# Tile loads of 192 rows on 64 partitions, in alternate halves of TensorE's rows, in a two-layer graph kernel

## The chip, the cores and the metric

The kernel runs on one core of a Trainium2 chip. The metric is the device time of one execution in microseconds; lower is better.

## What is computed

A graph network with two layers over 50,000 nodes and 50,000 edges, 128 channels, all in float32. The edges are sorted by destination.

```python
h = relu(layernorm(x))
# layer 0: edge features, message, sum over edges, MLP on nodes
ef  = ssp(gaussians(edge_weight) @ Wf1 + bf1) @ Wf2 + bf2      # ssp(v) = softplus(v) - log 2
agg = segment_sum((h @ W_lin.T)[src] * ef, dst, N)
x   = x + ssp(agg @ Wm1 + bm1) @ Wm2 + bm2
# layer 1: own row and the mean over neighbours
h   = relu(layernorm(x))
neigh = h[dst] @ W_neigh.T + b_neigh
x   = x + h @ W_self.T + b_self + segment_sum(neigh, src, N) / max(count(src), 1)
```

## The kernel before

The rows are padded to 98 quads of 512 rows; a quad is four tiles of 128. There are three stages. A short first stage counts and ranks the edges. The middle stage is one software pipeline, `over_steps`, of 98 + 18 steps. In step s each engine works on several quads at once: the edge part of quads s to s-3, the node part of quads s-7 to s-12, and the edge rows for layer 1 of quads s-15 to s-18. The last stage sums the rows of layer 1 by source.

The change is in the middle stage. Two groups of products there sum rows by a one-hot matrix that VectorE makes:

- `block_sums` (L1049) adds the messages of one tile of 128 destinations. SyncE loads 256 consecutive rows of the message table into `win`, two rows on each of 128 partitions, and `one_hots` (L821) makes `hot`. For each of the four tiles there are two products of 128 x 128 x 128, eight in all.
- `edge_rows` (L1061) picks for each edge the row of its destination from 256 rows in `hwin` by means of `hotT` (`edge_hots`, L849), again eight products.

Both write the same PSUM bank (`agg_ps` is also `rows_ps`). ScalarE copies it out in `evacuate` to `aggs` and in `rows_out` (L978). A float32 product of 128 columns stands in the trace as two records, each with its own weight load.

The order of work inside a step is written out by hand in each engine's `step`, and each engine goes through its list strictly in that order; semaphores hold it back. On TensorE (L1072) it is: self product of s-11, `block_sums` of s-8, MLP product of s-9, node product with Wm1, neighbour product of s-11, `filter_up` of s (50 rows of the edge basis by Wf1), `edge_rows` of s-17, transposes of s-10, `wlin` product of s-2, filter product and transposes of s-1. `product` begins with one matmul of 3 rows that adds the bias.

Three waits matter in what follows. `filter_up` of quad s writes the bank that `soften` has still to read for quad s-1, so it waits for that `soften` (output `su`). On VectorE (L863) this `soften` of s-1 stands late in step s: behind `node_out` of s-11 (L842, output `ys` or `y_kept`), `row_keys`, small operations and the four instructions of `node_norm` (output `comb`). And `node_out` of s-11 waits for the self product of s-11, with which TensorE begins the same step s.

Of the kernel before, what the change touches and what calls it, by code (L numbers as in the profile page):

```python
# [8 lines left out]
C = 128  # L9
P = 128  # L10
QT = 4
# [9 lines left out]
SPAN = 2 * P  # L21
# [127 lines left out]
def gnn_kernel(nc, ins, out_dram):  # L149
# [5 lines left out]
    with ExitStack() as ctx:  # L155
# [62 lines left out]
        iota2 = consts[:, 3 * P + 7:3 * P + 9]  # L218
        qbase = sb("qbase", [P, QUADS])
        firsts = sb("firsts", [P, TILES])  # L220
# [5 lines left out]
        reach = sb("reach", [P, TILES, 2])  # L226
# [4 lines left out]
        weights += [(qbase, "qbase"), (iota4, "iota4")]  # L231
# [39 lines left out]
        with ExitStack() as sems:  # L271
# [63 lines left out]
            @block.sync  # L335
            def _(sp):
                for t, a in ((cur[:], ins["dst_flat"][0:ROWS].rearrange("(p t) -> p t", p=P)),
                             (nxt[:], ins["dst_flat"][1:ROWS + 1].rearrange("(p t) -> p t", p=P)),
                             (ends[:, 0, :], ins["tile_first"].partition_broadcast(P)),
                             (ends[:, 1, :], ins["tile_last"].partition_broadcast(P)),  # L340
                             (first_row[0:1, :], ins["tile_first"].unsqueeze(0))):
                    sp.dma_start(t, a).then_inc(dst_loaded, 16)
                sp.dma_start(consts[:], ins["consts"]).then_inc(consts_loaded, 16)
                for t, name in weights:
                    sp.dma_start(t[:], ins[name]).then_inc(weights_loaded, 16)
                for t, name in rows:
# [4 lines left out]
                sp.dma_start(msg_dram[ROWS:ROWS + SPAN, :].rearrange("(p w) c -> p (w c)", p=P), pads[:, 0:2 * MW]).then_inc(pads_set, 16)  # L351
                sp.dma_start(h1_dram[ROWS:ROWS + SPAN, :].rearrange("(p w) c -> p (w c)", p=P), pads[:, 0:2 * C]).then_inc(pads_set, 16)
                sp.wait_ge(starts_ready, 1)
                sp.dma_start(off_dram.rearrange("(h l) -> h l", h=HI), starts[:]).then_inc(starts_out, 16)
                sp.wait_ge(starts_out, 16)
                sp.dma_start(start_row[0:1, :], off_dram.unsqueeze(0)).then_inc(starts_in, 16)
                sp.wait_ge(starts_in, 16)
                sp.wait_ge(pads_set, 16 * 3)
                sp.wait_ge(weights_loaded, 16 * (len(weights) + len(rows)))

            @block.vector
            def _(dve):
# [41 lines left out]
                for w in range(2):  # L404
                    nc.vector.tensor_scalar(reach[:, :, w], firsts[:], iota2[:, w:w + 1], None, ALU.add)
# [159 lines left out]
        rel = sb("rel", [P, QT, 2])  # L565
# [9 lines left out]
        with nc.If(unfit == 0), ExitStack() as fast:  # L575
# [9 lines left out]
            with ExitStack() as sems:  # L585
# [9 lines left out]
                win = st("win", [P, 2, QT, 2, MW])  # L595
                hwin = st("hwin", [P, 2, QT, 2, C])
                hot = st("hot", [P, QT, 2, P])
                hotT = st("hotT", [P, QT, 2, P])
                row_out = st("row_out", [P, 2, QT, RW])
                msgw = st("msgw", [P, 2, QT, MW])  # L600
                dst_keys = st("dst_keys", [P, 2, QROWS], i32)
# [24 lines left out]
                u_ps, turn_ps, proj_ps, filt_ps, agg_ps, nu_ps, mlp_ps, self_ps = bank  # L626
                neigh_ps, rows_ps = self_ps, agg_ps
# [4 lines left out]
                def _(sp):  # L632
# [29 lines left out]
                    def load_windows(j, par):  # L662
# [11 lines left out]
                        for k, start in enumerate(starts_of):  # L674
                            sp.dma_start(win[:, par, k, :, :].rearrange("p w c -> p (w c)"),
                                         msg_dram[bass.ds(start, SPAN), :].rearrange("(p w) c -> p (w c)", p=P)).then_inc(win_loaded[par], 16)

                    def load_keys(q, par):
                        if not at_first(q, 2):
                            sp.wait_ge(x_hot, q - 1)  # L680
                            hold(sp, sp_passed)
                        sp.dma_start(dst_keys[:, par, :], ins["dst_rows"][q, :].partition_broadcast(P)).then_inc(x_keys[par], 16)

                    def load_hidden(q, par):
# [11 lines left out]
                        for t, first in enumerate(firsts_of):  # L696
                            sp.dma_start(hwin[:, par, t, :, :].rearrange("p w c -> p (w c)"),
                                         h1_dram[bass.ds(first, SPAN), :].rearrange("(p w) c -> p (w c)", p=P)).then_inc(x_win[par], 16)
# [57 lines left out]
                def _(dve):  # L756
# [59 lines left out]
                    def window_dst(j, par):  # L816

                        dve.wait_ge(win_loaded[par], half_count(j, par, 64))
                        nc.vector.tensor_scalar(rel[:], win[:, par, :, :, C], qbase[:, bass.ds(j, 1)], None, ALU.subtract).then_inc(n_rel, 1)

                    def one_hots(j):  # L821

                        dve.wait_ge(n_rel, j + 1)
                        wait_used(dve, n_agg, j, 1)
                        nc.vector.tensor_tensor(hot[:], iota4[:].rearrange("p (t c) -> p t c", t=QT).unsqueeze(2).broadcast_to([P, QT, 2, P]),  # L825
                                                rel[:].unsqueeze(3).broadcast_to([P, QT, 2, P]), ALU.is_equal).then_inc(n_hot, 1)
# [22 lines left out]
                    def edge_hots(q, par):  # L849

                        dve.wait_ge(x_keys[par], half_count(q, par, 16))
                        wait_used(dve, x_sum, q, 1)
                        nc.vector.tensor_tensor(hotT[:], dst_keys[:, par, :].rearrange("p (t e) -> p t e", t=QT).unsqueeze(2).broadcast_to([P, QT, 2, P]),  # L853
                                                reach[:, bass.ds(QT * q, QT), :].unsqueeze(3).broadcast_to([P, QT, 2, P]), ALU.is_equal).then_inc(x_hot, 1)
# [8 lines left out]
                    def step(s, even, odd, pair, slot, late):  # L863
                        if there(s - 8):
                            one_hots(s - 8)
# [59 lines left out]
                def _(act):  # L925
# [52 lines left out]
                    def rows_out(q, par):  # L978
# [4 lines left out]
                        nc.scalar.activation(row_out[:, par, :, 0:C], rows_ps[:].rearrange("p (t c) -> p t c", t=QT), ACT.Copy).then_inc(x_rows, 1)  # L983

                    nc.scalar.preload_act_table_set("natural_log_exp_and_others")  # L985
                    def step(s, even, odd, pair, slot, late):
                        if there(s - 9):
                            evacuate(s - 9, aggs[:], agg_ps[:], n_agg, n_u, n_aggT)
# [7 lines left out]
                        if there(s - 9):  # L996
                            clamp(s - 9, nu_ps[:], bm1_top, nclamp[:], n_u, n_clamp)
                        if there(s - 11):
                            evacuate(s - 11, nhT[:], turn_ps[:], n_turned, n_neigh, n_hT, ACT.Relu)
                        if there(s - 12):  # L1000
                            hidden_out(s - 12, even)
                        if there(s - 18):
                            rows_out(s - 18, even)
# [22 lines left out]
                def _(pe):  # L1026
# [22 lines left out]
                    def block_sums(j, par):  # L1049
# [3 lines left out]
                        if there(j - 10):  # L1053
                            pe.wait_ge(x_rows, j - 10 + 1)
                        for k in range(QT):
                            for w in range(2):
                                last = nc.tensor.matmul(agg_ps[:, k * P:(k + 1) * P], win[:, par, k, w, 0:C], hot[:, k, w, :],  # L1057
                                                        start=(w == 0), stop=(w == 1))
                        last.then_inc(n_agg, 1)

                    def edge_rows(q, par):  # L1061
# [4 lines left out]
                        for t in range(QT):  # L1066
                            for w in range(2):
                                last = nc.tensor.matmul(rows_ps[:, t * P:(t + 1) * P], hotT[:, t, w, :], hwin[:, par, t, w, :],  # L1068
                                                        start=(w == 0), stop=(w == 1))
# [1023 lines left out]
```

## Time and profile before

| what | us |
|---|---|
| median of 3 runs | 1956.16 (1955.95 to 1958.92) |
| the profiled execution, its own time | 1953.39 |
| its span | 1950.9 |
| steps 17 to 97 of the middle stage, in the span | 402.66 to 1468.32 |
| TensorE busy, share of the span | 90% |
| VectorE, ScalarE, GpSimd busy | 77%, 54%, 52% |

The span is what the profile shows of the execution. A step's length is read as the distance from one bias matmul of the self product to the next. Busy shares are averages over stages; which engine bounds a step is read from the timeline of that step.

### The profile page before, as it was taken

How to read it: one execution, taken by the hardware profiler on the slowest of the kernel's cores; microseconds unless marked ns; L12 is line 12 of the kernel's file. 1: busy time of each engine (PE TensorE's matmuls, PEld its weight loads, DVE VectorE, ACT ScalarE, POOL GpSimd, SP SyncE). 2: the span in 40 equal slices, each digit the busy share in tenths (PEclk: the TensorE clock that was granted, in tenths of full speed). 3: DMA queues.
4: the chain of work that ended last, by engine and by line, in shares of the span. 5: the costliest groups of instructions: out<-in, count | busy, mean ns of one | idle time of the engine just before them, and what ended most of it. 6: DMA issues, size and time to landing. Idle time of an engine off the chain costs nothing. (4 is left out here: it accounts for less than half of the span.)

```text
span 1950.9 us, 46269 instructions
## 1 busy us (share of the span) xinstructions
PE 1751.3 (90%) x11686; PEld 1336.5 (69%) x11686; DVE 1495.5 (77%) x4726; ACT 1062.0 (54%) x2453; POOL 1021.4 (52%) x886
## 2 busy tenths in 40 slices
PE   2639868999999999999999999999999864988997
PEld 1212236777777777777777777777777754888897
DVE  8989946887778778777877777787787624777886
ACT  1000067777777777777777777777775311333333
POOL 0000054346666666666666666666663363765776
PEclk9769968999999999999999999999999977999999
DMA  2000035677777777778778777777776655999876
GB/s 78 0 0 1 6 79 150 179 228 226 228 235 237 224 227 234 225 227 239 233 222 234 233 208 209 219 213 202 215 213 196 179 170 167 283 283 279 261 219 177
DMA packets 342165, 372.51 MB, mean 191 GB/s; under 512 B 40509, under 2 KB 269759, under 8 KB 342079
## 3 DMA queue, kind: packets, MB, share of 16 engines
q1 hardware_dynamic: 265246, 293.99, 51.9%
q0 software_dynamic: 25088, 51.83, 9.0%
q10 hardware_dynamic: 51744, 25.70, 4.4%
q8 instruction: 35, 0.57, 0.1%
q14 instruction: 52, 0.42, 0.1%
HBM read 251.54 MB, written 119.82 MB: 190 GB/s over the span
## 5 line engine op out<-in xcount | busy, mean ns | idle before, releaser
L730 POOL DMA_INDIRECT xg<-in_x,srcs x392 | 432.2, 1102 | 606.0 <-issue 281.9
L741 POOL DMA_INDIRECT row_table<-row_out,posq x392 | 382.5, 976 | 195.4 <-issue 126.7
L1197 PE MATMUL psum<-bin_rows,bin_hot 128*128 128x129 f32 x2352 | 286.5, 279 | 46.4 <-DVE bin_hot L1170 46.0
L1197 PEld LDWEIGHTS psum<-bin_rows,bin_hot 128*128 128x128 f32 x2352 | 271.3, 192 | 61.6 <-issue 33.0
L1068 PEld LDWEIGHTS psum<-hwin,hotT 128*128 128x128 f32 x1568 | 190.6, 199 | 76.0 <-issue 68.3
L853 DVE TENSOR_TENSOR hotT<-dst_keys,reach 128x1024 f32<-128x1024 int32 x98 | 120.7, 1232 | 141.7 <-PE psum L1068 141.7
L970 ACT ACTIVATE nhT<-psum 128x512 f32<-128x512 f32 x98 | 58.5, 597 | 308.8 <-PE psum L1040 301.9
L1068 PE MATMUL psum<-hwin,hotT 128*128 128x128 f32 x1568 | 208.4, 288 | 13.0 <-DMA hwin<-h_table 5.9
L1057 PE MATMUL psum<-hot,win 128*128 128x128 f32 x1568 | 192.9, 277 | 3.4 <-DVE hot L825 3.4
L1057 PEld LDWEIGHTS psum<-hot,win 128*128 128x128 f32 x1568 | 184.3, 193 | 4.1 <-DVE hot L825 4.1
L1170 DVE TENSOR_TENSOR bin_hot<-iota,bin_rel 128x1536 f32<-128x1536 f32 x98 | 174.3, 1779 | 5.3
L1032 PE MATMUL psum<-bias,ones 3*128 3x512 bf16 x392 | 151.7, 387 | 12.8 <-ACT h1s L976 9.9
L964 ACT ACTIVATE xn<-xg,shift,rstd 128x128 f32<-128x128 f32 x392 | 161.0, 493 | 0.0
L1047 PE MATMUL psum<-basis,wf 50*128 50x512 f32 x196 | 114.9, 667 | 23.8 <-DVE su L802 17.5
L1212 ACT ACTIVATE x<-psum,inverse 128x128 f32<-128x128 f32 x200 | 57.0, 368 | 132.4 <-DVE inverse L1180 122.0
L1032 PEld LDWEIGHTS psum<-bias,ones 3*128 3x128 bf16 x392 | 35.5, 91 | 127.5 <-issue 89.1
L825 DVE TENSOR_TENSOR hot<-iota,rel 128x1024 f32<-128x1024 f32 x98 | 117.6, 1200 | 4.0 <-issue 4.0
L985 ACT ACT_TABLE_LOAD x1 | 1.3, 1283 | 214.1 <-PEq L271 214.1
L1034 PE MATMUL psum<-wf,su 128*128 128x128 f32 x784 | 117.2, 294 | 0.0
L1034 PE MATMUL psum<-wneigh,nhT 128*128 128x128 f32 x784 | 114.0, 289 | 0.0
L1034 PEld LDWEIGHTS psum<-wf,su 128*128 128x128 f32 x784 | 98.1, 196 | 23.0 <-issue 23.0
L1034 PE MATMUL psum<-wself,nhT 128*128 128x128 f32 x784 | 113.5, 288 | 0.0
(169 smaller groups left out, 3648.8 us busy)
## 6 DMA issues: line engine op xcount, KB each, us to landing
win<-msg_table SPq DMA_DIRECT2D x392, 129.0 KB
hwin<-h_table SPq DMA_DIRECT2D x392, 128.0 KB
bin_rows<-row_table SPq DMA_DIRECT2D x196, 195.0 KB, 3.2
msg_table<-msgw SPq DMA_DIRECT2D x98, 258.0 KB
nx<-in_x_nodes SPq DMA_DIRECT2D x98, 256.0 KB
h_table<-h1s SPq DMA_DIRECT2D x98, 256.0 KB
dst_keys<-in_dst_rows SPq DMA_DIRECT2D x98, 256.0 KB
y_table<-ys SPq DMA_DIRECT2D x61, 256.0 KB, 4.3
```

Of the source, the lines that this page charges most:

```text
L730: nc.gpsimd.indirect_dma_start(out=xg[:, par, t, :], out_offset=None, in_=ins["x"], in_offset=bass.IndirectOffsetOnAxis(ap=srcs[:, par, t: ...
L741: nc.gpsimd.indirect_dma_start(out=row_dram, out_offset=bass.IndirectOffsetOnAxis(ap=posq[:, par, t:t + 1], axis=0), in_=row_out[:, par, t ...
L825: nc.vector.tensor_tensor(hot[:], iota4[:].rearrange("p (t c) -> p t c", t=QT).unsqueeze(2).broadcast_to([P, QT, 2, P]), rel[:].unsqueeze( ...
L853: nc.vector.tensor_tensor(hotT[:], dst_keys[:, par, :].rearrange("p (t e) -> p t e", t=QT).unsqueeze(2).broadcast_to([P, QT, 2, P]), reach ...
L964: last = nc.scalar.activation(out[:, t, :], source[:, t, :], ACT.Relu, bias=shift_[:, t:t + 1], scale=rstd_[:, t:t + 1])
L1032: nc.tensor.matmul(ps[:], ones3[0:3, :], bias3[0:3, b, :], start=True, stop=False)
L1034: last = nc.tensor.matmul(ps[:, t * P:(t + 1) * P], left[:, t * P:(t + 1) * P], weights_[:], start=(b is None), stop=(b is None or t == QT ...
L1047: nc.tensor.matmul(u_ps[:], wf1[at:at + BASIS, :], basis[at:at + BASIS, slot, :], start=True, stop=True).then_inc(e_u, 1)
L1057: last = nc.tensor.matmul(agg_ps[:, k * P:(k + 1) * P], win[:, par, k, w, 0:C], hot[:, k, w, :], start=(w == 0), stop=(w == 1))
L1068: last = nc.tensor.matmul(rows_ps[:, t * P:(t + 1) * P], hotT[:, t, w, :], hwin[:, par, t, w, :], start=(w == 0), stop=(w == 1))
L1170: nc.vector.tensor_tensor(bin_hot[:, par, :, :, :], iota4[:].rearrange("p (b n) -> p b n", b=2).unsqueeze(2).broadcast_to([P, 2, BTILES, B ...
L1197: last = nc.tensor.matmul(bank[2 * slot + b][:, h * MW:(h + 1) * MW], bin_hot[:, slot % 2, b, w, h * P:(h + 1) * P], bin_rows[:, slot, b, ...
```

## The change

`win` and `hwin` now take 192 rows of a tile, three rows on each of 64 partitions. Tiles 0 and 2 of a quad lie in partitions 0 to 63, tiles 1 and 3 in partitions 64 to 127. A tile then needs three products with 64 rows of contraction instead of two with 128: twelve in a group instead of eight, and neighbours in the order alternate between the lower and the upper 64 rows of TensorE. The two halves write to different banks: each of banks 4 and 5 holds two tiles of the sums in its left half and two tiles of the edge rows in its right half, so the waits between `block_sums` and `edge_rows` over a shared bank are gone. To free that bank, the MLP, self and neighbour products share one bank (`node_ps`), with waits of each for the reader of the one before. `hot` and `hotT` have 768 columns instead of 1024 and two buffers each. The keys come in two loads of 64 partitions and half the bytes. In the first stage `reach` is made by six instructions on 64 partitions instead of two on 128. The order in the step changes too.

```diff
-SPAN = 2 * P
+HALF = P // 2
+WT = 3
+SPAN = WT * HALF
...
-                u_ps, turn_ps, proj_ps, filt_ps, agg_ps, nu_ps, mlp_ps, self_ps = bank
-                neigh_ps, rows_ps = self_ps, agg_ps
+                u_ps, turn_ps, proj_ps, filt_ps, _, _, nu_ps, node_ps = bank
+                self_ps = mlp_ps = neigh_ps = node_ps
+                agg_at, rows_at = 0, 2 * P
...
+                def tile_ps(at, t):
+
+                    return bank[4 + t % 2][:, at + t // 2 * P:at + t // 2 * P + P]
...
-                            sp.dma_start(win[:, par, k, :, :].rearrange("p w c -> p (w c)"),
-                                         msg_dram[bass.ds(start, SPAN), :].rearrange("(p w) c -> p (w c)", p=P)).then_inc(win_loaded[par], 16)
+                            sp.dma_start(win[half_of(k), par, k // 2, :, :].rearrange("p w c -> p (w c)"),
+                                         msg_dram[bass.ds(start, SPAN), :].rearrange("(p w) c -> p (w c)", p=HALF)).then_inc(win_loaded[par], 16)
...
-                        wait_used(dve, n_agg, j, 1)
+                        wait_used(dve, n_agg, j, 2)
...
-                        wait_used(dve, x_sum, q, 1)
+                        wait_used(dve, x_sum, q, 2)
...
-                        if there(j - 10):
-                            pe.wait_ge(x_rows, j - 10 + 1)
-                        for k in range(QT):
-                            for w in range(2):
-                                last = nc.tensor.matmul(agg_ps[:, k * P:(k + 1) * P], win[:, par, k, w, 0:C], hot[:, k, w, :],
-                                                        start=(w == 0), stop=(w == 1))
+                        for g in range(2):
+                            for w in range(WT):
+                                for h in range(2):
+                                    last = nc.tensor.matmul(tile_ps(agg_at, 2 * g + h), win[half_of(h), par, g, w, 0:C], hot[half_of(h), par, g, w, :],
+                                                            start=(w == 0), stop=(w == WT - 1))
...
                         if there(s - 11):
                             wait_used(pe, n_hn, s - 11, 1)
+                            if at_first(s - 11, 1):
+                                pe.wait_ge(n_x1, s - 10 + 1)
                             product(s - 11, self_ps, nhT, wself, 2, n_hT, n_y, n_self)
                         if there(s - 8):
                             block_sums(s - 8, even)
+                        if there(s):
+                            filter_up(s, even, pair, slot)
                         if there(s - 9):
+                            if there(s - 11):
+                                pe.wait_ge(n_y, s - 11 + 1)
                             product(s - 9, mlp_ps, nsu, wm2, 1, n_soft, n_x1, n_mlp)
...
+                        if there(s - 17):
+                            edge_rows(s - 17, odd)
                         if there(s - 11):
                             pe.wait_ge(n_y, s - 11 + 1)
+                            if there(s - 9):
+                                pe.wait_ge(n_x1, s - 9 + 1)
                             product(s - 11, neigh_ps, nhT, wneigh, 3, n_hT, n_hn, n_neigh)
-                        if there(s):
-                            filter_up(s, even, pair, slot)
-                        if there(s - 17):
-                            if there(s - 8):
-                                pe.wait_ge(n_aggT, s - 8 + 1)
-                            edge_rows(s - 17, odd)
```

TensorE, one step of the middle stage before, from the bias of the self product on. `basis,wf` is `filter_up`, `hot,win` is `block_sums`, `hwin,hotT` is `edge_rows`; the semaphore `a_e_soft` counts the `soften` of the edge part.

```order
L1032 MATMUL psum<-bias,ones 128x512 [waits a_n_y,a_n_hT,a_n_hn]
L1034 MATMUL psum<-wself,nhT 128x128 x4
L1057 MATMUL psum<-hot,win 128x128 [waits a_n_aggT,a_x_rows,a_win_loaded0,a_n_hot]
L1057 MATMUL psum<-hot,win 128x128 x7
L1032 MATMUL psum<-bias,ones 128x512 [waits a_n_x1,a_n_soft]
L1034 MATMUL psum<-wm,nsu 128x128 x4
L1083 MATMUL psum<-aggs,wm 128x512 [waits a_n_soft,a_n_aggT]
L1032 MATMUL psum<-bias,ones 128x512 [waits a_n_hn,a_n_hT,a_n_y]
L1034 MATMUL psum<-wneigh,nhT 128x128 x4
L1047 MATMUL psum<-basis,wf 128x512 [waits a_e_soft,a_basis_ready]
L1068 MATMUL psum<-hwin,hotT 128x128 [waits a_x_win1,a_x_rows,a_x_hot,a_n_aggT]
L1068 MATMUL psum<-hwin,hotT 128x128 x7
```

The same step in the changed kernel:

```order
L1055 MATMUL psum<-bias,ones 128x512 [waits a_n_y,a_n_hT,a_n_hn]
L1057 MATMUL psum<-wself,nhT 128x128 x4
L1079 MATMUL psum<-hot,win 128x128 [waits a_n_aggT,a_win_loaded1,a_n_hot]
L1079 MATMUL psum<-hot,win 128x128 x11
L1070 MATMUL psum<-basis,wf 128x512 [waits a_e_soft,a_basis_ready]
L1055 MATMUL psum<-bias,ones 128x512 [waits a_n_x1,a_n_soft,a_n_y]
L1057 MATMUL psum<-wm,nsu 128x128 x4
L1112 MATMUL psum<-aggs,wm 128x512 [waits a_n_soft,a_n_aggT]
L1091 MATMUL psum<-hwin,hotT 128x128 [waits a_x_rows,a_x_win0,a_x_hot]
L1091 MATMUL psum<-hwin,hotT 128x128 x11
L1055 MATMUL psum<-bias,ones 128x512 [waits a_n_hT,a_n_hn,a_n_x1,a_n_y]
L1057 MATMUL psum<-wneigh,nhT 128x128 x4
```

`filter_up` moves from the eighth place of the step to the third, right behind `block_sums`; `edge_rows` moves ahead of the neighbour product.

ScalarE, the same part of a step before (`nhT` is the copy of the transposed hidden rows, `h1s` that of the neighbour product):

```order
L970 ACTIVATE efb<-psum 128x512 [waits a_e_msg,a_e_filter]
L964 ACTIVATE xn<-xg,shift,rstd 128x128 [waits a_e_turned,a_e_shift]
L964 ACTIVATE xn<-xg,shift,rstd 128x128 x3
L941 ACTIVATE nclamp<-psum,cols 128x512 [waits a_n_u]
L970 ACTIVATE nhT<-psum 128x512 [waits a_n_neigh,a_n_turned]
L976 ACTIVATE h1s<-psum 128x512 [waits a_h1_stored0,a_n_neigh]
L983 ACTIVATE row_out<-psum 128x4x128 [waits a_scattered0,a_x_ones,a_x_sum]
L955 ACTIVATE lnv<-emv,cols 128x4 [waits a_e_aggr]
```

And in the changed kernel:

```order
L993 ACTIVATE efb<-psum 128x512 [waits a_e_msg,a_e_filter]
L987 ACTIVATE xn<-xg,shift,rstd 128x128 [waits a_e_turned,a_e_shift]
L987 ACTIVATE xn<-xg,shift,rstd 128x128 x3
L964 ACTIVATE nclamp<-psum,cols 128x512 [waits a_n_u]
L1006 ACTIVATE row_out<-psum 128x2x2x128 [waits a_scattered0,a_x_ones,a_x_sum]
L999 ACTIVATE h1s<-psum 128x512 [waits a_h1_stored0,a_n_neigh]
L993 ACTIVATE nhT<-psum 128x512 [waits a_n_neigh,a_n_turned]
L978 ACTIVATE lnv<-emv,cols 128x4 [waits a_e_aggr]
```

The two copies `row_out` and `h1s` now stand ahead of `nhT`. VectorE's order within a step is the same in both kernels.

## Rows read from the trace of the kernel before

**Rows 1.** The page: its first line, and busy time, share, instructions by engine.

```profile
span 1950.9 us, 46269 instructions
PE 1751.3 (90%) x11686; PEld 1336.5 (69%) x11686; DVE 1495.5 (77%) x4726; ACT 1062.0 (54%) x2453; POOL 1021.4 (52%) x886
```

**Rows 2.** Stretches: length, busy time (instructions) by engine, granted clock, DMA share, GB/s.

```profile
402.66:1468.32 1065.66, 1065.66 (x7130) 822.76 (x7129) 837.22 (x3317) 771.94 (x1701) 674.79 (x642) 1.00 0.76 224
1468.32:1552.46 84.14, 76.79 (x550) 62.22 (x550) 61.06 (x200) 39.33 (x82) 30.45 (x32) 1.00 0.67 197
```

**Rows 3.** Timeline of TensorE, one step: start us, duration us, line, operation, shapes, records.

```profile
1008.05 0.39 PE L1032 MATMUL psum<-bias,ones 3*128 3x512 bf16 x1
1008.36 1.16 PE L1034 MATMUL psum<-wself,nhT 128*128 128x128 f32 x8
1009.36 1.95 PE L1057 MATMUL psum<-hot,win 128*128 128x128 f32 x16
1011.24 0.38 PE L1032 MATMUL psum<-bias,ones 3*128 3x512 bf16 x1
...
1012.55 1.02 PE L1083 MATMUL psum<-aggs,wm 128*128 128x512 f32 x2
1013.50 0.38 PE L1032 MATMUL psum<-bias,ones 3*128 3x512 bf16 x1
1013.82 1.16 PE L1034 MATMUL psum<-wneigh,nhT 128*128 128x128 f32 x8
1014.91 1.12 PE L1047 MATMUL psum<-basis,wf 50*128 50x512 f32 x2
1015.96 2.05 PE L1068 MATMUL psum<-hwin,hotT 128*128 128x128 f32 x16
1017.85 0.60 PE L1040 MATMUL psum<-ident,comb 128*128 128x128 f32 x4
...
1021.12 0.39 PE L1032 MATMUL psum<-bias,ones 3*128 3x512 bf16 x1
```

**Rows 4.** Timeline of VectorE in the same step.

```profile
1009.63 0.69 DVE L847 TENSOR_TENSOR ys<-psum,x 128x512 f32<-128x512 f32 x1
...
1010.65 1.11 DVE L833 TENSOR_SCALAR comb<-x,nmv,nsmall 128x128 f32<-128x128 f32 x4
...
1011.81 0.75 DVE L802 SCALAR_TENSOR_TENSOR su<-psum,cols,lu 128x512 f32<-128x512 f32 x1
```

**Rows 5.** Timeline of ScalarE, with the idle time ahead in brackets.

```profile
1005.41 0.60 ACT L970 ACTIVATE nhT<-psum 128x512 f32<-128x512 f32 x1 [3.02 <-PE psum L1040]
1005.91 0.59 ACT L976 ACTIVATE h1s<-psum 128x512 f32<-128x512 f32 x1
...
1010.12 0.72 ACT L950 ACTIVATE lu<-eu,cols 128x512 f32<-128x512 f32 x1
...
1024.50 0.71 ACT L950 ACTIVATE lu<-eu,cols 128x512 f32<-128x512 f32 x1
```

**Rows 6.** Groups by line and shape: total busy us, mean ns | idle us before.

```profile
L1068 PEld LDWEIGHTS psum<-hwin,hotT 128*128 128x128 f32 x1568 | 190.6, 199 | 76.0 <-issue 68.3 <-DVE hotT L853 7.7
L1047 PE MATMUL psum<-basis,wf 50*128 50x512 f32 x196 | 114.9, 667 | 23.8 <-DVE su L802 17.5 <-ACT basis L936 6.1
L1083 PE MATMUL psum<-aggs,wm 128*128 128x512 f32 x196 | 104.4, 614 | 1.1 <-ACT aggs L970 1.1
```

**Rows 7.** Timeline of TensorE: starts of steps 11, 17, 98, and two of the drain.

```profile
335.22 0.39 PE L1032 MATMUL psum<-bias,ones 3*128 3x512 bf16 x1
...
402.66 0.39 PE L1032 MATMUL psum<-bias,ones 3*128 3x512 bf16 x1
...
1468.32 0.39 PE L1032 MATMUL psum<-bias,ones 3*128 3x512 bf16 x1
...
1500.80 0.39 PE L1032 MATMUL psum<-bias,ones 3*128 3x512 bf16 x1 [1.18 <-ACT h1s L976]
...
1511.13 0.38 PE L1032 MATMUL psum<-bias,ones 3*128 3x512 bf16 x1 [1.18 <-ACT h1s L976]
```

More of the change, by code:

```diff
@@ L230, in gnn_kernel @@
         iota4 = sb("iota4", [P, QROWS])
-        weights += [(qbase, "qbase"), (iota4, "iota4")]
+        weights += [(qbase, "qbase"), (qhalf, "qhalf"), (iota4, "iota4")]
         bf1_top, bf1_low, bm1_top, bm1_low = (cols[:, k:k + 1] for k in (5, 6, 7, 8))
@@ L403, in _ @@
                 link(nc.vector.tensor_reduce(out=violations[:, 4:5], in_=bad[:], axis=AX.X, op=ALU.add))
-                for w in range(2):
-                    nc.vector.tensor_scalar(reach[:, :, w], firsts[:], iota2[:, w:w + 1], None, ALU.add)
+                for h in range(2):
+                    half = slice(HALF * h, HALF * h + HALF)
+                    for w in range(WT):
+                        nc.vector.tensor_scalar(reach[half, :, w], firsts[half, :].rearrange("p (g h) -> p h g", h=2)[:, h, :],
+                                                iota3[half, w:w + 1], None, ALU.add)
                 link(nc.vector.tensor_tensor(bad[:], curf[:], nxtf[:], ALU.is_gt))
@@ L593, in st @@
                     return sems.enter_context(nc.sbuf_tensor(name, shape, dt))
[L595 to L598, printed above, removed]
+                win = st("win", [P, 2, 2, WT, MW])
+                hwin = st("hwin", [P, 2, 2, WT, C])
+                hot = st("hot", [P, 2, 2, WT, P])
+                hotT = st("hotT", [P, 2, 2, WT, P])
                 row_out = st("row_out", [P, 2, QT, RW])
                 msgw = st("msgw", [P, 2, QT, MW])
-                dst_keys = st("dst_keys", [P, 2, QROWS], i32)
+                dst_keys = st("dst_keys", [P, 2, 2 * P], i32)
                 aggs = st("aggs", [P, QROWS])
@@ L681, in load_keys @@
                             hold(sp, sp_passed)
-                        sp.dma_start(dst_keys[:, par, :], ins["dst_rows"][q, :].partition_broadcast(P)).then_inc(x_keys[par], 16)
+                        for h in range(2):
+                            sp.dma_start(dst_keys[half_of(h), par, :], ins["dst_halves"][q, h, :].partition_broadcast(HALF)).then_inc(x_keys[par], 16)
                     def load_hidden(q, par):
@@ L696, in load_hidden @@
                         for t, first in enumerate(firsts_of):
-                            sp.dma_start(hwin[:, par, t, :, :].rearrange("p w c -> p (w c)"),
-                                         h1_dram[bass.ds(first, SPAN), :].rearrange("(p w) c -> p (w c)", p=P)).then_inc(x_win[par], 16)
+                            sp.dma_start(hwin[half_of(t), par, t // 2, :, :].rearrange("p w c -> p (w c)"),
+                                         h1_dram[bass.ds(first, SPAN), :].rearrange("(p w) c -> p (w c)", p=HALF)).then_inc(x_win[par], 16)
                     def step(s, even, odd, pair, slot, late):
@@ L864, in step @@
                         if there(s - 8):
-                            one_hots(s - 8)
+                            one_hots(s - 8, even)
                         if there(s - 17):
@@ L997, in step @@
                             clamp(s - 9, nu_ps[:], bm1_top, nclamp[:], n_u, n_clamp)
+                        if there(s - 18):
+                            rows_out(s - 18, even)
+                        if there(s - 12):
+                            hidden_out(s - 12, even)
                         if there(s - 11):
                             evacuate(s - 11, nhT[:], turn_ps[:], n_turned, n_neigh, n_hT, ACT.Relu)
[L1000 to L1003, printed above, removed]
                         if there(s - 1):
@@ L1065, in edge_rows @@
                         wait_used(pe, x_rows, q, 1)
[L1066 to L1069, printed above, removed]
+                        for g in range(2):
+                            for w in range(WT):
+                                for h in range(2):
+                                    last = nc.tensor.matmul(tile_ps(rows_at, 2 * g + h), hotT[half_of(h), par, g, w, :], hwin[half_of(h), par, g, w, :],
+                                                            start=(w == 0), stop=(w == WT - 1))
                         last.then_inc(x_sum, 1)
@@ L2057 @@
         "qbase": np.broadcast_to((QROWS * np.arange(QUADS)).astype(np.float32), (P, QUADS)),
+        "qhalf": (QROWS * np.arange(QUADS)[None] + P * (np.arange(P)[:, None] // HALF)).astype(np.float32),
+        "dst_halves": dst_pad.reshape(QUADS, 2, 2, P).transpose(0, 2, 1, 3).reshape(QUADS, 2, 2 * P),
         "iota4": np.broadcast_to(np.arange(QROWS, dtype=np.float32), (P, QROWS)),
```

40 lines of the change are left out of this document (24 added, 16 removed).

## The prediction

> **What bounds the kernel now.** I read the shares by engine first [rows 1]: TensorE is busy 90% of the span, VectorE 77%. Shares alone do not tell what a wait costs, so I took the stretches next. From 402.66 to 1468.32 us, which is steps 17 to 97 [rows 7], TensorE has no idle time at all: 1065.66 us busy of 1065.66, at the full granted clock of 1.00 [rows 2]. VectorE is busy 837 us of these and ScalarE 772. So 1065.66 / 81 = 13.16 us per step, and in this stretch every microsecond added to TensorE's list, or waited in it, is one of the total. The timeline of one step [rows 3] gives 13.07 us from 1008.05 to 1021.12; the mean is 0.09 more, for a few waits here and there, which I leave as they are.
>
> From the starts in [rows 3] I take the parts of a step: self product with its bias 1.31 (1008.05 to 1009.36), block sums 1.88, MLP product with bias 1.31, Wm1 product 0.95, neighbour bias 0.32 and product 1.09, `filter_up` 1.05, edge rows 1.89, and from the first transpose to the next step 3.27. They add up to 13.07.
>
> **The products.** Before, a group has 16 records in 1.88 us, 0.1175 each [rows 3]. After, it has 24 records of 64 rows. The trace of before does not show two products in different halves of the rows one upon the other, so I bound it. Fewer rows do not make a record shorter: 512 columns with 50 rows take 667 ns and with 128 rows 614 [rows 6]. At the upper end nothing overlaps and a group takes 24 x 0.1175 = 2.82 us. At the lower end each half runs beside the other; 12 records stand behind each other in a half, the second half is one record late, and it takes 13 x 0.1175 = 1.53 us. A group of another number of rows than its neighbours also costs a little at its border: the neighbour product takes 1.09 ahead of the 50 rows of `filter_up`, the self product 1.00 ahead of 128 rows [rows 3]. I add 0.09 for the edge rows, which leave and enter such borders, and in place of the one that `filter_up` has now. So a group of edge rows is 1.62 or 2.91 us. I take the lower value, because loads are already well hidden here: 16 weight loads of 199 ns mean [rows 6] pass within a group of 1.88, so the engine does run several things at a time.
>
> The Trainium skill, "TensorEngine Tiling (Array Packing)", under Key Properties, says that different tiles of the array can load weights and multiply in parallel. By that rule a group takes 1.62 us, and no row here shows it. The Trainium skill, "TensorE: Matmul & The Clock Gate", Part 3, says that a weight load overlaps with a matmul in flight only when their row groups differ. The trace does not agree: [rows 6] and [rows 3] have loads of all 128 rows beside matmuls of all 128 rows, since 16 loads of 199 ns alone would be 3.2 us in a group that takes 1.88. By that rule the new groups would gain even more than the overlap I count; I do not count it.
>
> **The order.** Here lies the larger term. `filter_up` of quad s waits for `su` of s-1. Before it stands 6.86 us into the step (1014.91 less 1008.05), after `su` is done at 1011.81 + 0.75 = 1012.56, which is 4.51 into the step [rows 3, 4]; 2.35 us of slack. After the change it stands behind the self product and the block sums: 1.31 + 0.09 + 1.53 = 2.93 us into the step. And `su` cannot come earlier by much. It is the end of a chain that starts with the same step's self product: the self product ends at 1008.36 + 1.16 = 1009.52, 1.47 into the step; `node_out` needs it (0.05 for the signal); from the start of `node_out` at 1009.63 to the end of `su` at 1012.56 VectorE works 2.93 us without a gap [rows 3, 4], and its order is unchanged; 0.05 more for the signal back. That is 1.47 + 0.05 + 2.93 + 0.05 = 4.50 us. So TensorE stands still for 4.50 - 2.93 = 1.57 us in each step, and everything behind `filter_up` in its queue, which is all the rest of the step and the next self product, waits with it. The loop is closed: self product, `node_out`, `su`, `filter_up`, rest of the step, next self product.
>
> The new step: 4.50, then `filter_up` 1.05, MLP 1.31, Wm1 0.95, edge rows 1.62, neighbour bias and product 0.32 + 1.00 (no border behind it now), the rest 3.27. The sum is 14.02 us, against 13.07. That the block sums became cheaper buys nothing: they lie under the wait. 81 steps x 0.95 = +77 us.
>
> **What the other edits cost.** Each of these I count at nothing, with its cover. ScalarE must have `lu` ready for `su`: it ended 2.79 us into the step (1010.84), with the edge basis made in between 4.09 (1025.21 less 1021.12) [rows 3, 5]. After the change `h1s` and `row_out` are copied in the 3.02 us for which ScalarE waited ahead of `nhT` [rows 5], so `lu` comes about 1 us earlier in relation to the transposes, and is due only at 4.50 - 0.80 = 3.70. Without that cover the basis steps would lose up to 0.4 us each, 16 us in all. The waits over the shared bank: the MLP product now asks for `node_out`, which is done some 2.2 us before `su` [rows 4]; the neighbour product asks for the residual, which follows the MLP product directly on VectorE (a sum of 512 columns like `node_out`, 0.69 us [rows 4]), while TensorE has 0.95 + 1.62 us of other work in between; the next self product asks for `h1s`, with 3.27 us in between. VectorE's one-hots shrink by a quarter, and with two buffers no longer wait for TensorE, but VectorE does not bound the step outside of the chain. SyncE issues one more load per step; loads move fewer bytes, and the DMA engines are busy 0.76 now [rows 2]. GpSimd's gathers and scatters keep their place and have more time. The first stage gets four more small instructions on VectorE, under 1 us.
>
> **The ends of the pipeline.** Steps 11 to 16 have no edge rows and last (402.66 - 335.22) / 6 = 11.24 us [rows 7]. After, VectorE's chain is 0.13 shorter (no `row_keys`): 4.37 + 1.05 + 1.31 + 0.95 + 1.32 + 3.27 = 12.27. That is 6 x 1.03 = +6 us. Steps 98 to 105 have no `filter_up`, so no such wait. They last 10.33 us (1500.80 to 1511.13), with 1.18 us idle for `h1s` [rows 7]. There the move of `h1s` ahead of `nhT` saves its 0.59, and the two groups 0.3 less borders: about -0.8 each, -6 us.
>
> The sum on the profiled execution: 1953.4 + 77 + 6 - 6 = 2030 us. The median of the runs is 2.8 above the profiled execution, so I forecast 2033 us.
>
> **The rivals.**
>
> *The halves do not overlap.* Then a group is 2.82 to 2.91 us. The block sums would mostly hide under the wait (1.31 + 0.09 + 2.82 = 4.22 of 4.50), and the step is 14.02 + 1.29 = 15.31, that is 81 x 2.24 = +181 us, +6 in steps 11 to 16, and in the drain some 8 x 1.7 + 6 x 1.2 = +20. That gives 1953.4 + 207 + 2.8 = 2163 us. For it speaks that a float32 product is two records that follow in the same half, so the other half's work must be taken past a waiting record, and no row shows that. Values in between are possible: each 0.1 us of a group is 8 us.
>
> *The wait does not arise, and the kernel is faster.* If `su` were there when TensorE comes to `filter_up`, a step would be 2.93 + 7.90 + 1.62 = 12.45 us, 81 x 0.62 = -50, and the time 1953.4 - 50 - 2 - 6 + 2.8 = 1898 us. The point from which this side begins is `su` at 13.07 - 7.90 - 1.62 = 3.55 us into the step instead of 4.50; VectorE's chain would have to lose 0.95 of its 2.93 us. Nothing in it is touched, and all of it is busy time. It also needs that the halves overlap.
>
> *The change does nothing.* The order of waits hides under something I misread, and overlap and wait cancel: 1956 us. For a tie the group of edge rows would have to take 0.67 us, or the chain be as above.
>
> *The granted clock falls.* TensorE would idle 1.57 us in 14.0. From 1468.32 to 1552.46 it idles 84.14 - 76.79 us in pieces of 1.18 and the clock stays 1.00 [rows 2, 7]; longer pieces are not shown in this part. If it fell to 1.2 GHz in places, the time goes above 2200 us.
>
> **How the numbers follow.** Overlap with the wait 0.52, forecast 2033. Halves apart or mostly apart 0.38, 2163. Faster 0.04, no change 0.02, lower clock 0.04. The range takes in both of the first two: at the low end an overlap with no late record (1.41 us, -10) and a drain gain twice mine (-6), 2012; at the high end 2163 with 17 for basis steps that wait for ScalarE, 2180. A difference within 0.2% is about what a measurement of this kernel cannot tell from none. Faster 0.04, same 0.02, slower 0.94.
>
> **What would show it.** In the profile after: an idle time of about 1.5 us on TensorE ahead of `basis,wf`, put down to VectorE `su`, in each step; a distance of 14.0 us between self products; `hwin,hotT` with 24 records in about 1.6 us where halves overlap, 2.9 where they do not; VectorE idle ahead of `node_out`; ScalarE without its wait of 3 us ahead of `nhT` but with waits ahead of `row_out` and `h1s`. Wrong would be a chain from self product to `su` shorter than 3.5 us, or any step under 13 us.

## The result, and the profile after

The changed kernel takes 2067.16 us (median of 4 runs, 2063.55 to 2068.13) against 1956.39 us for the kernel before on the same chip. The ratio is 1.056, with a 95% interval of 1.054 to 1.058: clearly slower. The forecast was 2033 us with a range of 2012 to 2180.

The page of the changed kernel answers to [rows 1]. TensorE has fallen from 90% to 83% of a longer span, and its busy time fell too, although it has 1568 more records:

```profile
span 2065.3 us, 49732 instructions
...
PE 1716.9 (83%) x13254; PEld 1273.2 (62%) x13254; DVE 1447.4 (70%) x4730; ACT 1083.0 (52%) x2453; POOL 982.7 (48%) x886
```

One step on TensorE, the counterpart of [rows 3] (timeline: start us, duration us, line, operation, records, and in brackets the idle time ahead and who ended it):

```profile
1052.02 0.39 PE L1055 MATMUL psum<-bias,ones 3*128 3x512 bf16 x1
1052.34 1.16 PE L1057 MATMUL psum<-wself,nhT 128*128 128x128 f32 x8
...
1053.42 1.61 PE L1079 MATMUL psum<-hot,win 64*128 64x128 f32 x24
...
1056.60 1.12 PE L1070 MATMUL psum<-basis,wf 50*128 50x512 f32 x2 [1.57 <-DVE su L825]
...
1059.92 1.61 PE L1091 MATMUL psum<-hwin,hotT 64*128 64x128 f32 x24
...
1061.46 0.38 PE L1055 MATMUL psum<-bias,ones 3*128 3x512 bf16 x1
...
1066.04 0.39 PE L1055 MATMUL psum<-bias,ones 3*128 3x512 bf16 x1
```

The step is 1066.04 - 1052.02 = 14.02 us where it was 13.07. The edge rows, 24 records of 64 rows, take 1061.46 - 1059.92 = 1.54 us where 16 records of 128 rows took 1.89. And there is a stop of 1.57 us ahead of `basis,wf`, which is `filter_up`. VectorE in the same step, the counterpart of [rows 4]:

```profile
1053.60 0.69 DVE L870 TENSOR_TENSOR ys<-psum,x 128x512 f32<-128x512 f32 x1 [0.77 <-PE psum L1057]
...
1054.63 1.13 DVE L856 TENSOR_SCALAR comb<-x,nmv,nsmall 128x128 f32<-128x128 f32 x4
...
1055.81 0.74 DVE L825 SCALAR_TENSOR_TENSOR su<-psum,cols,lu 128x512 f32<-128x512 f32 x1
```

The self product ends at 1052.34 + 1.16 = 1053.50. VectorE had been waiting for it (0.77 us idle, which it was not in [rows 4]), starts `node_out` 0.10 us later and ends `su` at 1056.55; TensorE goes on at 1056.60, 4.58 us into the step.

Not all steps are 14.0 us. In the 81 steps 17 to 97 (421.36 to 1584.74 us) 17 last 15.55 to 15.85 us; the others last 13.93 to 14.25, 14.02 in the mean. One of the 17 begins at 1137.67. Its stretches (length, busy time by engine with instructions, granted clock, DMA share, GB/s):

```profile
1137.67:1141.00 3.33, 3.01 (x34) 2.47 (x33) 2.56 (x12) 2.09 (x4) 2.22 (x3) 1.00 0.59 156
...
1144.00:1148.00 4.00, 4.00 (x25) 2.50 (x26) 2.90 (x19) 0.69 (x1) 2.63 (x3) 0.59 0.71 236
1148.70:1153.28 4.58, 4.58 (x36) 3.84 (x35) 2.56 (x9) 3.58 (x10) 3.31 (x4) 1.00 0.38 117
```

TensorE's timeline there:

```profile
1142.23 1.12 PE L1070 MATMUL psum<-basis,wf 50*128 50x512 f32 x2 [1.55 <-DVE su L825]
...
1144.60 1.79 PE L1112 MATMUL psum<-aggs,wm 128*128 128x512 f32 x2
1146.32 2.46 PE L1091 MATMUL psum<-hwin,hotT 64*128 64x128 f32 x24
```

From 1144 to 1148 the granted clock averages 0.59, which is mostly the lower of its two levels, 1.2 GHz in place of 2.4. In all 17 steps it goes down 1.9 to 2.5 us after the stop has ended and stays down for 3.4 us. The Wm1 product takes 1.79 us where it takes 1.02 elsewhere, and the edge rows are slower too. The Trainium skill, "TensorE: Matmul & The Clock Gate", puts drops of the clock in the middle of a kernel down to long idle gaps between bursts of matmuls (closing table). The trace shows that shorter ones can do it too: the gaps here are 1.48 to 1.80 us, one in each step, and the clock falls.

Where the 114.4 us of span went (2065.3 - 1950.9), by the starts of steps in both traces:

| part | before | after | difference |
|---|---|---|---|
| up to step 11 | 335.22 | 339.05 | +3.8 |
| steps 11 to 16 | 67.4 | 82.3 | +14.9 |
| steps 17 to 97 | 1065.7 | 1163.4 | +97.7 |
| step 98 to the first product of the last stage | 163.5 | 152.7 | -10.9 |
| last stage | 319.1 | 327.9 | +8.8 |

The last row can't be put down to the products: nothing in that stage is different, and in the profiled executions of the experiments below it lasts between 323.8 and 329.8 us, also in the one that keeps the 256 rows (327.9). Why it was 319.1 in the trace before stays open. Nor is the first row shown to be the stop's doing: step 11 begins between 333.7 and 340.2 us in those executions, at 337.4 in one without any stop and at 336.3 in one with it.

### The profile page after: what moved, and what is told of

It reads as the page before. It is cut to its first block and busy times, and to the rows that moved or that the text cites. A ratio compares the mean times of both kernels' runs of the same rounds, so it can differ in the third digit from the quotient of the medians.

```text
span 2065.3 us, 49732 instructions
## 1 busy us (share of the span) xinstructions
PE 1716.9 (83%) x13254; PEld 1273.2 (62%) x13254; DVE 1447.4 (70%) x4730; ACT 1083.0 (52%) x2453; POOL 982.7 (48%) x886
## 5 line engine op out<-in xcount | busy, mean ns | idle before, releaser
L863 DVE TENSOR_TENSOR x<-psum,nx 128x512 f32<-128x512 f32 x98 | 67.8, 692 | 247.5 <-issue 241.0
L1091 PEld LDWEIGHTS psum<-hwin,hotT 64*128 64x128 f32 x2352 | 156.6, 208 | 95.5 <-issue 91.7
L1091 PE MATMUL psum<-hwin,hotT 64*128 64x128 f32 x2352 | 175.7, 301 | 13.6 <-DMA hwin<-h_table 8.8
L964 ACT ACTIVATE nclamp<-psum,cols 128x512 f32<-128x512 f32 x98 | 67.3, 687 | 197.0 <-PE psum L1112 193.1
L1079 PE MATMUL psum<-hot,win 64*128 64x128 f32 x2352 | 157.7, 280 | 2.0 <-DVE hot L848 2.0
L1079 PEld LDWEIGHTS psum<-hot,win 64*128 64x128 f32 x2352 | 138.9, 187 | 14.1 <-DVE hot L848 2.4
L1006 ACT ACTIVATE row_out<-psum 128x512 f32<-128x512 f32 x98 | 58.6, 598 | 130.9 <-PE psum L1091 119.0
L1112 PE MATMUL psum<-aggs,wm 128*128 128x512 f32 x196 | 119.3, 695 | 0.0
L1057 PE MATMUL psum<-wm,nsu 128*128 128x128 f32 x784 | 118.6, 296 | 0.0
L836 DVE TENSOR_TENSOR msgw<-psum,efb 128x512 f32<-128x512 f32 x98 | 67.7, 690 | 71.1 <-PE psum L1057 70.6
```

The costliest lines, as they stand in the source:

```text
L863: nc.vector.tensor_tensor(flat(x1, par), mlp_ps[:], flat(nx, par), ALU.add).then_inc(n_x1, 1)
L1057: last = nc.tensor.matmul(ps[:, t * P:(t + 1) * P], left[:, t * P:(t + 1) * P], weights_[:], start=(b is None), stop=(b is None or t == QT ...
L1079: last = nc.tensor.matmul(tile_ps(agg_at, 2 * g + h), win[half_of(h), par, g, w, 0:C], hot[half_of(h), par, g, w, :], start=(w == 0), stop ...
L1091: last = nc.tensor.matmul(tile_ps(rows_at, 2 * g + h), hotT[half_of(h), par, g, w, :], hwin[half_of(h), par, g, w, :], start=(w == 0), sto ...
```

## The experiments

Two theories had to be told apart from rivals. The *wait theory*: the products in two halves are a gain, and the new place of `filter_up` is the loss. The *overlap theory*: the gain of the products comes from halves that run side by side. Then a third question, what makes the clock fall.

**`filter_up` back in its old place.** The changed kernel with this edit alone:

```diff
-                        if there(s):
-                            filter_up(s, even, pair, slot)
                         if there(s - 9):
...
                             product(s - 11, neigh_ps, nhT, wneigh, 3, n_hT, n_hn, n_neigh)
+                        if there(s):
+                            filter_up(s, even, pair, slot)
```

> The changed kernel with filter_up back behind the neighbour product; all else as changed. Wait theory: the stop ahead of filter_up (1.5 us per step in the changed kernel) is the whole loss, the products themselves are a gain. A step is then 0.31 + 1.09 (self) + 1.54 (sums) + 1.31 + 0.95 + 1.54 (edge rows) + 1.40 (neighbour) + 1.05 + 3.27 = 12.46 us, against 13.07 in the kernel before, and no step is stretched to 15.65: about 1900 us, ratio 0.97. Rival, another wait takes over (shared bank, VectorE): 13.1 us or more per step, ratio 1.00 or above. Rival, the stretched steps come from the 64-row products and not from the stop: they stay, one in 5 or 6 with 1.6 us more, about 1925 us.

Measured: 1903.44 us, ratio 0.971 (0.969 to 0.974). All 81 steps last 12.52 or 12.53 us. TensorE and the clock in a stretch of full steps:

```profile
450.00:1400.00 950.00, 950.00 (x7895) 708.31 (x7893) 743.50 (x3106) 745.89 (x1595) 625.59 (x607) 1.00 0.72 204
```

No idle time, full clock, no stretched step. The kernel before took 1960.8 us beside these runs, so the ratios are the fairer measure: 1.056 less 0.971 of 1956 us, that is some 166 us, is the cost of the moved `filter_up`, and all the rest of the change together is worth 0.029, some 56 us. No other wait took the place of the one removed, and the 64-row products alone do not bring the clock down.

**The order alone.** The kernel before, in which only `filter_up` moves:

```diff
                             block_sums(s - 8, even)
+                        if there(s):
+                            filter_up(s, even, pair, slot)
...
                             product(s - 11, neigh_ps, nhT, wneigh, 3, n_hT, n_hn, n_neigh)
-                        if there(s):
-                            filter_up(s, even, pair, slot)
```

> The kernel before with only filter_up moved to the place that the change gives it, right behind the block sums; 256 rows, 128 partitions, one bank as before. Wait theory: the same chain from the self product to su holds it, 4.50 us into the step, where TensorE comes at 1.31 + 1.88 + 0.09 = 3.28: a stop of 1.2 us, a step of 4.50 + 1.05 + 1.31 + 0.95 + 1.89 + 1.32 + 3.27 = 14.29 us, 81 x 1.22 = +99 us, about 2060 us with the first steps, ratio 1.05. If the stop alone makes the clock fall for a while, the stretched steps (one in 5 or 6, 1.6 us more) show here too and it is 2085 us. If the products are what costs in the changed kernel, it stays near 1956 us.

Measured: 2137.01 us, ratio 1.090 (1.087 to 1.093).

```profile
1023.09 1.95 PE L1057 MATMUL psum<-hot,win 128*128 128x128 f32 x16
1026.38 1.12 PE L1047 MATMUL psum<-basis,wf 50*128 50x512 f32 x2 [1.34 <-DVE su L802]
...
450.00:1400.00 950.00, 855.81 (x5527) 648.31 (x5526) 650.42 (x2575) 605.17 (x1317) 515.60 (x502) 0.95 0.68 198
```

The stop is there with 128-row products too, so it belongs to the order. Every second full step lasts 14.3 us at full clock, as worked out (14.29). The others last 14.5 to 14.6, with a stop of 1.54 to 1.67 us, because in them ScalarE's `lu` comes after VectorE could have taken it. In one of them:

```profile
799.66 0.75 DVE L802 SCALAR_TENSOR_TENSOR su<-psum,cols,lu 128x512 f32<-128x512 f32 x1 [0.16 <-ACT lu L950]
```

And 34 of the 81 steps 17 to 97 are stretched to 15.87 us or more, twice as many as in the changed kernel, and most of steps 11 to 16 besides. That is the larger part of what my number for this run missed: 34 x 1.58 = 54 us.

**The halves in turn.** `filter_up` in its old place, and in both groups the order of loops changed, so that the three products of one tile follow each other in one half:

```diff
-                            for w in range(WT):
-                                for h in range(2):
+                            for h in range(2):
+                                for w in range(WT):
```

> As the run with filter_up behind the neighbour product, but in each group of products the three of one tile follow each other in the same half of the rows, before the other half has its three. Overlap theory: halves run beside each other only where they alternate; a group of 24 records goes from 1.5 us towards 24 x 0.1175 = 2.8 us, a step by up to 2.6 us, to about 2110 us. Rival: the engine takes the other half's products past the waiting ones, the group stays near 1.5 to 1.6 us and the time that of the alternating run.

Measured: 1962.3 us, ratio 1.001 (0.999 to 1.003); steps of 13.18 us.

```profile
1013.72 1.93 PE L1091 MATMUL psum<-hwin,hotT 64*128 64x128 f32 x24
1015.59 0.38 PE L1055 MATMUL psum<-bias,ones 3*128 3x512 bf16 x1
```

A group takes 1.87 us: between the two answers I had expected. Either six records of one half and six of the other still overlap for a part, or a record of 64 rows is shorter in itself.

**All in one half.** `filter_up` in its old place, and all twelve products of a group read the lower 64 partitions:

```diff
-                                    last = nc.tensor.matmul(tile_ps(agg_at, 2 * g + h), win[half_of(h), par, g, w, 0:C], hot[half_of(h), par, g, w, :],
+                                    last = nc.tensor.matmul(tile_ps(agg_at, 2 * g + h), win[half_of(0), par, g, w, 0:C], hot[half_of(0), par, g, w, :],
...
-                                    last = nc.tensor.matmul(tile_ps(rows_at, 2 * g + h), hotT[half_of(h), par, g, w, :], hwin[half_of(h), par, g, w, :],
+                                    last = nc.tensor.matmul(tile_ps(rows_at, 2 * g + h), hotT[half_of(0), par, g, w, :], hwin[half_of(0), par, g, w, :],
```

> As the run with filter_up behind the neighbour product, but all twelve products of both groups read the lower 64 partitions (so the sums of tiles 1 and 3 are not those of their own rows; the work is the same in number and shape). It takes away the other half for all of the group. Overlap theory: 24 records in one half take 24 x 0.1175 = 2.8 us, a step 12.52 + 2 x 1.28 = 15.1 us, the time about 2110 us. Rival, to which the 1.87 us of the halves in turn point: a record of 64 rows is itself shorter than one of 128 (0.078 us), and the group stays at 1.9 us, the time near 1962 us.

Measured: one run of 2157.87 us.

```profile
1012.03 2.94 PE L1091 MATMUL psum<-hwin,hotT 64*128 64x128 f32 x24
1014.91 0.38 PE L1055 MATMUL psum<-bias,ones 3*128 3x512 bf16 x1
```

The group takes 2.88 us, 0.12 per record, as with 128 rows; the step is 15.19 us. So a 64-row record is not shorter: the whole gain is overlap of the halves, and alternating makes it nearly complete (1.54 of 2.88). In turn, 0.33 of the 1.34 us is lost again (1.87). The one half was read with neighbours writing to two banks, as in the alternating order, so different banks alone do not give the overlap; whether it needs them was not tried. My 2110 us was low because I counted only the full steps; the groups also run in the steps of the fill and the drain (12.1 to 12.4 us there, instead of 9.5 to 11.1).

**The chain on VectorE.** The changed kernel, `filter_up` where the change has it, but `su` made earlier:

```diff
+                        if there(s - 1):
+                            soften(s - 1, u_ps[:], bf1_low, ln_out[:], su[:], e_softln, e_filter, e_soft)
                         if there(s - 7):
                             window_dst(s - 7, odd)
...
                             mean_shift(s - 1, emv[:, odd, :, :], rstd[:], shift[:], e_rstd, e_shift)
-                            soften(s - 1, u_ps[:], bf1_low, ln_out[:], su[:], e_softln, e_filter, e_soft)
```

> The changed kernel, with filter_up where the change puts it, but VectorE makes su of the edge part ahead of window_dst, node_norm and mean_shift instead of behind them. Chain theory: VectorE's chain from the end of the self product to su loses 0.15 + 1.02 + 0.15 = 1.3 us, so su is ready 3.2 us into the step (in every second step, with the edge basis, ScalarE's lu can be the later one, 3.2 to 3.9), the stop shrinks from 1.54 to 0.2 to 0.9 us, the step to 12.7 to 13.4 us and the time to 1915 to 1970 us. Rival, the stop is not due to this chain: no change from 2067 us.

Measured: 1997.33 us, ratio 1.018 (1.016 to 1.021). At full clock the steps alternate between 12.7 and 13.45 us. TensorE and VectorE:

```profile
1013.58 1.12 PE L1071 MATMUL psum<-basis,wf 50*128 50x512 f32 x2 [0.26 <-issue]
...
1026.22 0.75 DVE L825 SCALAR_TENSOR_TENSOR su<-psum,cols,lu 128x512 f32<-128x512 f32 x1 [0.65 <-issue]
...
1027.02 1.12 PE L1071 MATMUL psum<-basis,wf 50*128 50x512 f32 x2 [1.00 <-DVE su L825]
```

The steps came out as the chain says: a stop of 0.26 us in one step and of 1.00 in the next, where ScalarE's `lu` (1025.48 to 1026.19, behind the edge basis) is the last to come. The total missed my range of 1915 to 1970, again by the clock: 27 steps, all of them with the stop of 1.00 us or just under, are stretched to about 15.07 us, which is 27 x 1.6 = 43 us.

**The stop filled with work.** The changed kernel with the block sums done twice:

```diff
-                        for g in range(2):
-                            for w in range(WT):
-                                for h in range(2):
+                        for again in range(2):
+                            for g in range(2):
+                                for w in range(WT):
+                                    for h in range(2):
...
```

> The changed kernel with the group of block sums done twice over (the same products into the same places again): 1.5 us more work for TensorE per step, right where it stands still for 1.54 us. Clock theory: the stretched steps (20 of 81, 1.6 us each) come from the stop itself; with the stop filled the step stays 14.0 us, none is stretched, and the time falls by about 30 us to 2035 us although there is more work. Rival: the stretched steps have another cause (the 64-row products, the 50-row product): they stay, 2067 us; and if the stop was not free, it is 2067 + 81 x 1.5 = 2190 us.

Measured: 2046.27 us, ratio 1.043 (1.041 to 1.046), which is 21 us less than the changed kernel (25 by the ratios) with some 1.3 us more work per step.

```profile
1018.64 2.95 PE L1080 MATMUL psum<-hot,win 64*128 64x128 f32 x48
1021.77 1.12 PE L1070 MATMUL psum<-basis,wf 50*128 50x512 f32 x2 [0.18 <-DVE su L825]
...
450.00:1400.00 950.00, 934.25 (x8683) 721.79 (x8683) 667.92 (x2786) 665.87 (x1423) 561.91 (x543) 1.00 0.63 184
```

The full steps stay at 13.94 to 14.30 us, the stop has shrunk to 0.15 to 0.51 us, none is stretched, and the clock is 1.00. This shows two things at once: work under the stop is free, and the low clock comes from the stop. The fall in time is smaller than the 30 us I expected, since the doubled group does cost where there is no stop: steps after the last `filter_up` take 10.77 us here and 9.46 in the changed kernel.

**`filter_up` behind the edge rows.** What the experiments point to: no stop, and the 50-row product beside 64-row products.

```diff
-                        if there(s):
-                            filter_up(s, even, pair, slot)
                         if there(s - 9):
...
                             edge_rows(s - 17, odd)
+                        if there(s):
+                            filter_up(s, even, pair, slot)
```

> The changed kernel with filter_up right behind edge_rows, ahead of the neighbour product, 6.7 us into the step: su is ready at 4.5, so there is no stop; and the 50 rows of filter_up follow 64-row products, as the change wants it, with no border of shapes between. Wait theory: a step of 12.52 - 0.09 = 12.43 us, full clock, about 1895 us, ratio 0.968. If the border costs nothing: 1903 us, as with filter_up behind the neighbour product.

Measured: 1869.99 us, ratio 0.9545 (0.9525 to 0.9564). Full steps last 12.18 us.

```profile
1014.20 1.61 PE L1091 MATMUL psum<-hwin,hotT 64*128 64x128 f32 x24
1015.65 1.02 PE L1070 MATMUL psum<-basis,wf 50*128 50x512 f32 x2
1016.60 0.39 PE L1055 MATMUL psum<-bias,ones 3*128 3x512 bf16 x1
1016.92 1.16 PE L1057 MATMUL psum<-wneigh,nhT 128*128 128x128 f32 x8
1017.91 0.60 PE L1063 MATMUL psum<-ident,comb 128*128 128x128 f32 x4
```

This beats both kernels. The gain over the old place of `filter_up` is 0.34 us per step, four times what I had expected from one border. From the starts: edge rows 1.45 (1.54 there), `filter_up` 0.95 (1.05), neighbour bias and product 1.31 (1.41), and the transposes and what follows 3.27 (3.33). So the parts beside a border between 128 rows and 50 or 64 seem to cost 0.06 to 0.10 us more each, and this order has fewer such borders; from 64 rows to 50 none shows. This is read from the starts alone: no run changed a border and nothing else. The Trainium skill, "TensorEngine Tiling (Array Packing)", says under Key Properties that changing the tiling mode drains TensorE. The starts fit that, though they show no drain as such; it gives no figure, and here the parts differ by 0.06 to 0.10 us.

## Why the prediction was right, and where it was short

**What bounds it.** Right. TensorE has no slack, and the time follows its list and its stops.

**The products.** Right on the side chosen. I put a group at 1.53 us plus 0.09 for borders, 1.62, and it takes 1.54. The range of 2012 to 2180 held both sides, so that the total lies in it says nothing on this point; the 24 records in 1.54 us do. (Its low end was added up wrongly: 2033 - 10 - 6 is 2017.) The half-by-half bound of 2.82 is confirmed by the run in one half (2.88). The argument that I gave for the choice, loads hidden behind matmuls, was weak: it says nothing on two matmuls at a time. That it came out on this side was luck as far as that argument goes; the choice was settled only by the runs.

**The order.** Right, and the larger term, as forecast. I put the stop at 1.57 us and it is 1.48 to 1.80 in the 81 steps, 1.56 in the middle; in the step shown `filter_up` starts 4.58 us into the step for my 4.50, mostly because `node_out` starts 0.10 and not 0.05 after the self product ends. The step is 14.02 us for my 14.02, which is luck: the 0.08 late and the 0.08 saved at the edge rows cancel. The run with the order alone, the run with `filter_up` put back and the run with a shorter chain each show the same cause.

**The other edits at nothing.** Right: put back, `filter_up` leaves a step without any idle time. ScalarE's cover held: its waits now stand ahead of `row_out` (0.94 us) and `h1s` (0.80), and `lu` ends 3.2 us into the steps with an edge basis, where 3.70 was enough. In the run with the order alone, which keeps the old order of copies, `lu` ends 3.9 to 4.1 us into them and each loses about 0.3 us, close to the 0.4 at most that I gave for a missing cover. In the run with `su` early the new order did not suffice either, and `lu` was late by 0.65 us in every second step, as the order of ScalarE's work makes one expect.

**The ends.** In the drain the steps last 9.46 us for the 10.33 before, as forecast. Steps 11 to 16 cost 14.9 us more and not 6: at full clock they last 12.40 us for my 12.27, and there too the clock fell, in four of the six (the longest is 15.52 us), for 7.9 us in all. Step 11 begins 3.8 us later than before, in first steps that I had not looked at; as said above, the cause of that is not shown.

**The granted clock.** This is the step that failed, in size. I took 1.00 throughout, on the strength of the drain before, where TensorE idles 1.18 us in every 10.33 at full clock, and gave a fall of the clock 0.04 as a case by itself, at over 2200 us. It came on top of the forecast case instead, and cost far less: 17 stretched steps x 1.63 = 28 us in steps 17 to 97, and 8 us in steps 11 to 16. The trace of before would have warned me 3 us behind where I stopped reading (1552.46). There TensorE stops for 1.34 us, and soon after its clock falls, so that `edge_rows` takes 3.15 us for 1.95 to 2.05 elsewhere:

```profile
1555.28 0.39 PE L1032 MATMUL psum<-bias,ones 3*128 3x512 bf16 x1 [1.34 <-DVE nsu L802]
...
1558.42 3.15 PE L1068 MATMUL psum<-hwin,hotT 128*128 128x128 f32 x16
```

The stretch that holds it:

```profile
1557.00:1562.00 5.00, 5.00 (x29) 4.77 (x28) 2.46 (x12) 0.00 (x0) 1.17 (x2) 0.66 0.35 112
```

The mean of the step before also held 0.09 us of small irregularities, 7 us in 81 steps, which I kept in the sum and which the new kernel does not have. Together: 28 + 9 in steps 11 to 16 (8 of the clock, 1 of the longer step) + 4 at the start + 9 of the last stage - 7 - 5 in the drain makes 38, and the difference to be explained is 114.4 - 77 = 37 us.

What stays open is why the clock falls in one step and not in the next. It is not the length of the stop alone. Of the 81 steps 17 to 97, 17 were hit with stops of 1.48 to 1.80 us, 34 with stops of 1.34 to 1.67 us and the 128-row products, and 27 with stops of 1.00 and 0.26 us by turns. In the drain before, stops of 1.18 us ahead of the self product hit none of five steps; in the next, with a second stop of 1.34 us, the clock fell, and in the same step of the changed kernel, with a second stop of 1.50 us, it did not. What stands around the stop, or when it comes, may matter, and no run here separates these.

The new order of ScalarE's copies was not tried by itself in the changed kernel: with the two groups in shared banks the old order leaves a read of a bank and a write to it unordered.

## What to carry to other kernels

Two groups of products with half the rows run side by side when neighbours in the order alternate between the halves; here they also wrote to different banks, and whether that is needed was not tried. Order them so, and try work of few rows next to each other. But before moving an operation ahead in an engine's list, follow the wait that it carries to the end of the other engine's list: here the wait closed a loop through VectorE that began at the same step's first product, and it cost three times what the rest of the change gained. If a stop in TensorE can't be avoided, its price is its length and, now and then, some microseconds at half clock, here 1.6 us each time; filling it with useless products was cheaper here than leaving it.

## What was not expected of the hardware

Halves overlap even where six records of one half follow each other: 24 records take 1.54 us alternating, 1.87 us in turn by six, and 2.88 us in one half. A float32 record of 128 columns costs 0.12 us with 64 rows as with 128. A stop of 1.0 to 1.8 us on TensorE, in each step of 14 to 14.6 us or in every second of 12.7 and 13.45, brought the granted clock down for 3.4 us in 17 to 34 of 81 steps, each time 1.3 to 2.5 us after TensorE had gone on, and repeated products in its place kept it at 1.00.
